# Gathering and transposing the rows of experts 2 to 8: parts of 128 in ten gathers and a block transpose on VectorE, for row gathers and TensorE transposes

## The reference

```python
S = jax.nn.softmax(layernorm(x) @ Wg, axis=-1)          # 1250 x 8
G, I = jax.lax.top_k(St, k)                             # k = 312 nodes for each expert
ex = jnp.take_along_axis(x[:, None], I[..., None], axis=2)       # rows of the normalised x
hmid = gelu(ex @ W1[e] + b1[e])                         # 312 x 512 by 512 x 1024, erf form
out = hmid @ W2[e] + b2[e]                              # 312 x 1024 by 1024 x 512
new_x = zeros.at[I].add(G[..., None] * out);  x = x + new_x
```

## Time and profile before

| | |
|---|---|
| median of 3 runs | 1441.53 us (1441.02 to 1441.79) |
| profiled execution's own time | 1442.35 us |
| its span | 1440.5 us |
| granted TensorE clock, mean over the span | 0.951 of full speed |
| PE busy | 1323.8 us, 92% |
| VectorE busy | 1027.4 us, 71% |
| ScalarE busy | 816.6 us, 57% |
| GpSimd busy | 799.3 us, 55% |
| expert stage | 1116.5 to 1440.5 us |

### The profile page before, as it was taken

One profiled execution on the slowest core, in us unless ns is written; L12 is line 12 of the kernel. 1 busy time (PEld: TensorE's weight loads), 2 busy tenths in 40 slices (PEclk: granted clock), 3 DMA queues, 4 the chain that ended last, 5 costly groups with the idle time before them and its releaser, 6 DMA issues. The chain is left out here.

```text
span 1440.5 us, 26692 instructions
## 1 busy us (share of the span) xinstructions
PE 1323.8 (92%) x7075; PEld 791.9 (55%) x7075; DVE 1027.4 (71%) x2512; ACT 816.6 (57%) x2049; POOL 799.3 (55%) x843
## 2 busy tenths in 40 slices
PE   5786799999999999999999999999962799999997
PEld 1463456656555556555555555555561455555553
DVE  7869589999999899999999999998776311111110
ACT  3769667777777777777777777777550111111111
POOL 5258577777777777777777777777200122222211
PEclk7689899999999999999999999999995799999998
DMA  7315033444443444444443333434452155555421
GB/s 246 162 44 162 20 113 113 123 130 123 126 127 110 129 124 127 127 132 136 123 115 109 110 114 109 115 109 112 65 189 71 58 164 163 163 163 162 145 37 18
DMA packets 65870, 172.45 MB, mean 120 GB/s; under 512 B 14260, under 2 KB 22820, under 8 KB 65191
## 3 DMA queue, kind: packets, MB, share of 16 engines
q0 software_dynamic: 43424, 105.53, 27.9%
q1 hardware_dynamic: 22398, 66.38, 13.4%
HBM read 148.53 MB, written 18.08 MB: 116 GB/s over the span
## 5 line engine op out<-in xcount | busy, mean ns | idle before, releaser
L1130 PE MATMUL PS<-prod,oneh 128*64 128x256 f32 x2052 | 469.6, 382 | 4.0 <-DVE region_s L944 2.0
L564 POOL DMA_INDIRECT recs<-rec_d,inv_i x342 | 323.2, 945 | 113.0 <-issue 81.0
L575 POOL DMA_INDIRECT gath<-table_d,recs x342 | 323.5, 946 | 106.0 <-issue 78.7
L1130 PEld LDWEIGHTS PS<-prod,oneh 128*64 128x64 f32 x2052 | 268.9, 137 | 199.4 <-issue 77.7
L707 ACT ACTIVATE oneh<-oneh,recs 128x64 f32<-128x64 f32 x1026 | 282.2, 338 | 145.7 <-DVE oneh L921 143.8
L1123 PE MATMUL PS<-prod,oneh 128*64 128x256 f32 x1368 | 356.1, 392 | 0.0
L1111 PE MATMUL PS<-wf_sb,h_t 128*128 128x512 f32 x684 | 333.2, 610 | 2.9 <-DVE h_t L907 2.9
L932 DVE TENSOR_TENSOR prod<-PS,gath 128x768 f32<-128x768 f32 x342 | 324.9, 950 | 0.0
L944 DVE TENSOR_TENSOR region_s<-region_s,PS 128x512 f32 x342 | 232.6, 680 | 17.9 <-issue 13.6
L714 ACT COPY PS<-c_rep 128x512 f32<-128x512 f32 x338 | 190.4, 583 | 79.0 <-DVE prod L932 78.6
L930 DVE TENSOR_TENSOR prod<-PS,gath 128x256 f32<-128x256 f32 x342 | 143.9, 421 | 54.6 <-DMA gath<-table_d,recs 38.7
(11 more groups left out here) (264 smaller groups left out, 1503.8 us busy)
## 6 DMA issues: line engine op xcount, KB each, us to landing
region_r<-wu SPq DMA_DIRECT2D x16, 512.0 KB, 4.3
region_r<-wd SPq DMA_DIRECT2D x16, 512.0 KB, 5.6
region_u<-wu SPq DMA_DIRECT2D x16, 512.0 KB, 4.3
region_u<-wd SPq DMA_DIRECT2D x16, 512.0 KB, 5.8
recs<-rec_d,inv_i POOLq DMA_INDIRECT x342, 2.6
gath<-table_d,recs POOLq DMA_INDIRECT x342, 3.3
region_u<-rec_in SPq DMA_DIRECT2D x1, 5168.0 KB, 16.1
rec_d<-region_u SPq DMA_DIRECT2D x1, 5168.0 KB
```

The source lines that it names most:

```text
L564: nc.gpsimd.indirect_dma_start(out=recs[:, q % RING, k, :], out_offset=None, in_=rec_d, in_offset=bass.IndirectOffsetOnAxis(ap=inv_i[:, t: ...
L575: nc.gpsimd.indirect_dma_start(out=gath[:, t % GRING, :], out_offset=None, in_=table_d, in_offset=bass.IndirectOffsetOnAxis(ap=recs[:, q % ...
L1130: return nc.tensor.matmul(to, oneh[:, slot, 1 + i, :], prod[:, slot, P_Q:P_B + i + 1:1 + i, :], start=i == 0, stop=i == 2, skip_group_chec ...
```

## The change

Experts are numbered from 0 in the code. Expert 0 keeps the row gathers and the transposes on PE. For experts 1 to 7:

- Ten gathers replace three. Each fetches 128 pieces of 128 values from `xn_d`, seen as 5000 rows of 128: 32 ranks times four parts, part a of a rank on partition 32a + rank. The index of a partition is 4 x node + part.
- For that, the node index of each rank has to stand on four partitions, 32 ranks to a column. VectorE masks the indices (`idx_b`), PE multiplies them by a constant matrix in two small float32 products with 8 and 2 moving columns (`spread_list`, placed behind row group 0 of the second layer), and VectorE forms `idx_t` (`take_parts`), which GpSimd waits for.
- One VectorE transpose in blocks of 32x32 turns the gathered parts into `ex_t`, straight from SBUF to SBUF, in place of 12 PE transposes and four copies.
- To make the blocks land where the first layer wants them, `xn_d` holds a row's features in another order: value m x 4 + k is feature k x 128 + m. ScalarE writes it so; expert 0's transposes read every fourth column.
- The constant matrix, the masks and the part numbers are made by eleven VectorE instructions at the start of the node stage. `ex_t` has 320 columns a slot, of which 312 are read.

```diff
@@ buffers
+BLOCK = 32
+GROUPS = -(-CAP // BLOCK)
+SLOTS = GROUPS * BLOCK
+        ex_parts = region_x[:, 0:2 * RCH * HID].rearrange("p (a h) -> p a h", a=2)[:, :, 0:GROUPS * FDIM].rearrange(
+            "p a (b h) -> p a b h", b=GROUPS)
+        xn_parts = xn_d.rearrange("n (a h) -> (n a) h", a=PARTS)
+        spread = prod_f[:, 0:2 * P].rearrange("p (n m) -> p n m", n=2)
...
@@ node stage, ScalarE
-                    nc.scalar.activation(xn[:, t, :], x1[:, t, :], ACT.Identity, bias=shift[0:BP, t:t + 1],
+                    nc.scalar.activation(xn[:, t, :].rearrange("p (m k) -> p k m", k=HK),
+                                         x1[:, t, :].rearrange("p (k m) -> p k m", k=HK),
+                                         ACT.Identity, bias=shift[0:BP, t:t + 1],
                                          scale=rstd[0:BP, 2, t:t + 1]).then_inc(n_xn, 1)
@@ node stage, VectorE
+                for part in range(PARTS):
+                    link(nc.vector.memset(part_of[part * BLOCK:(part + 1) * BLOCK, :], float(part)))
+                for n, (at, groups) in enumerate(((0, PARTS), (2 * P - ROW_AT[2], GROUPS - 2 * PARTS))):
+                    rows = ident[:, at:at + groups * BLOCK]
+                    link(nc.vector.tensor_reduce(spread[:, n, 0:BLOCK], rows.rearrange("p (q j) -> p j q", q=groups), AX.X,
+                                                 ALU.add))
+                    link(nc.vector.tensor_copy(spread[:, n, BLOCK:].rearrange("p (a j) -> p a j", j=BLOCK),
+                                               spread[:, n, 0:BLOCK].unsqueeze(1).to_broadcast([P, PARTS - 1, BLOCK])))
+                    link(nc.vector.tensor_reduce(own[:, 2 * PARTS * n:2 * PARTS * n + groups],
+                                                 rows.rearrange("p (q j) -> p q j", q=groups), AX.X, ALU.add))
+                link(nc.vector.tensor_copy(own[:, PARTS:2 * PARTS], own[:, 0:PARTS]))
@@ expert stage, GpSimd (expert 0: gather_rows, the three gathers as before)
+                def gather_parts(e, slot, first=False):
+                    if not first:
+                        pool.wait_ge(f_txe, HK + e - 2)
+                    hold(pool, l_parts, e, pool_passed)
+                    for b in range(GROUPS):
+                        nc.gpsimd.indirect_dma_start(
+                            out=ex_parts[:, slot, b, :], out_offset=None, in_=xn_parts,
+                            in_offset=bass.IndirectOffsetOnAxis(ap=idx_t[:, slot, b:b + 1], axis=0)
+                            ).then_inc(f_parts[slot], 16)
-                gather(0, 0)
-                gather(1, 1)
-                gather(2, 0)
+                gather_rows()
+                gather_parts(1, 1, first=True)
+                gather_parts(2, 0)
                 add_rows(0, 0)
...
@@ expert stage, VectorE, in take_list
+                    nc.vector.scalar_tensor_tensor(out=idx_f[:, :], in0=ex_list[:, slot, :, 0], scalar=float(BLOCKS),
                                                    in1=ex_list[:, slot, :, 1], op0=ALU.mult, op1=ALU.add).then_inc(l_idx, 1)
+                    dve.wait_ge(l_idx, e + 1)
+                    nc.vector.tensor_tensor(idx_b[:, 0:2 * PARTS].rearrange("p (c q) -> p c q", q=PARTS),
+                                            own[:, 0:2 * PARTS].rearrange("p (c q) -> p c q", q=PARTS),
+                                            idx_f[:, 0:2].unsqueeze(2).to_broadcast([P, 2, PARTS]), ALU.mult)
+                    nc.vector.tensor_scalar(idx_b[:, 2 * PARTS:], own[:, 2 * PARTS:], idx_f[:, 2:3], None, ALU.mult
+                                            ).then_inc(l_own, 1)
+                def take_parts(e, slot):
+                    dve.wait_ge(l_spread, e)
+                    nc.vector.scalar_tensor_tensor(out=idx_t[:, slot, :], in0=PS[:, 2, REC:REC + GROUPS],
+                                                   scalar=float(PARTS), in1=part_of[:, :].to_broadcast([P, GROUPS]),
+                                                   op0=ALU.mult, op1=ALU.add).then_inc(l_parts, 1)
+                def parts_transposed(slot, turns):
+                    dve.wait_ge(f_parts[slot], 16 * GROUPS * turns)
+                    nc.vector.transpose(ex_t[:, slot, :, :].rearrange("p k (b j) -> p b k j", b=GROUPS),
+                                        ex_parts[:, slot, :, :].rearrange("p b (i k) -> p b k i", k=HK)).then_inc(f_txe, 1)
...
@@ expert stage, VectorE, loop
                         rank_one_hots(2 * i + slot + 2)
-                        transposed(2 * i + slot + 1, 1 - slot)
+                        parts_transposed(1 - slot, i + 1)
                         take_list(2 * i + slot + 2, slot)
+                        take_parts(2 * i + slot + 2, slot)
                         take_gates(2 * i + slot + 1, 1 - slot)
                         biased(2 * i + slot, slot, i)
@@ expert stage, PE
-                                                   ex_rows[0:n, slot, c, k * P:(k + 1) * P], ident[0:n, 0:n])
+                        last = nc.tensor.transpose(PS[:, 6 + k % 2, at:at + n], ex_rows[0:n, 0, c, k:HID:HK], ident[0:n, 0:n])
+                def spread_list(e):
+                    pe.wait_ge(l_own, e + 1)
+                    for n, (at, end) in enumerate(((0, 2 * PARTS), (2 * PARTS, GROUPS))):
+                        last = nc.tensor.matmul(PS[:, 2, REC + at:REC + end], spread[:, n, :], idx_b[:, at:end],
+                                                start=n == 0, stop=True, skip_group_check=True)
+                    last.then_inc(l_spread, 1)
-                        if ahead is not None and f >= FK - HK:
-                            transpose_rows(e + 1, 1 - slot, ahead, f - (FK - HK))
@@ second layer, behind each row group
                         last.then_inc(f_dn, 1)
+                        if c == 0 and listed:
+                            spread_list(e + 2)
...
                 list_of(1)
+                spread_list(1)
                 for k in range(HK):
-                    transpose_rows(0, 0, 0, k)
+                    transpose_rows(k)
```

More of the change, by code:

```diff
@@ L358, in build @@
         l_gate = sem("l_gate")
+        l_own = sem("l_own")
+        l_spread = sem("l_spread")
+        l_parts = sem("l_parts")
         w_up = [sem("w_up0"), sem("w_up1")]
@@ L362, in build @@
         w_bd = [sem("w_bd0"), sem("w_bd1")]
-        f_rows = [[sem(f"f_rows{h}{c}") for c in range(RCH)] for h in range(2)]
+        f_rows = [sem(f"f_rows{c}") for c in range(RCH)]
+        f_parts = [sem(f"f_parts{h}") for h in range(2)]
         f_tx = sem("f_tx")
@@ L413, in build @@
         idx_add = sb("idx_add", [P, 2, RCH], I32)
+        idx_f = sb("idx_f", [P, RCH])
+        idx_b = sb("idx_b", [P, GROUPS])
+        spread = prod_f[:, 0:2 * P].rearrange("p (n m) -> p n m", n=2)
+        own = sb("own", [P, GROUPS])
+        idx_t = sb("idx_t", [P, 2, GROUPS], I32)
+        part_of = sb("part_of", [P, 1])
         def load_up(sp, e, slot, part):
@@ L1472, in _, with gather_rows @@
                 pool.sem_inc(f_free, 2)
-                def gather(e, slot):
-                    pool.wait_ge(f_tx, 4 * e + 4)
-                    hold(pool, l_idx, e + 1, pool_passed)
+                def gather_rows():
+                    hold(pool, l_idx, 1, pool_passed)
                     for c in range(RCH):
                         nc.gpsimd.indirect_dma_start(
-                            out=ex_rows[0:ROWS[c], slot, c, :], out_offset=None, in_=xn_d,
-                            in_offset=bass.IndirectOffsetOnAxis(ap=idx_e[0:ROWS[c], slot, c:c + 1], axis=0)
-                            ).then_inc(f_rows[slot][c], 16)
+                            out=ex_rows[0:ROWS[c], 0, c, :], out_offset=None, in_=xn_d,
+                            in_offset=bass.IndirectOffsetOnAxis(ap=idx_e[0:ROWS[c], 0, c:c + 1], axis=0)
+                            ).then_inc(f_rows[c], 16)
+                def gather_parts(e, slot, first=False):
[7 more added lines that the diff above has]
+                            ).then_inc(f_parts[slot], 16)
                 def add_rows(e, slot):
@@ L1504, in _ @@
                         e = 2 * i + 2 - slot
-                        gather(e + 2, slot)
+                        gather_parts(e + 2, slot)
                         add_rows(e, slot)
                         settle(e)
-                gather(EXPERTS - 1, 1)
+                gather_parts(EXPERTS - 1, 1)
                 for e in range(EXPERTS - 3, EXPERTS):
@@ L1538, in _ @@
             def _(dve):
-                dve.sem_inc(f_txe, 2)
                 dve.sem_inc(f_bias, 3)
@@ L1604, in _, with transpose_rows @@
                 pe.wait_ge(g_list, 1)
-                pe.sem_inc(f_tx, 8)
                 pe.sem_inc(f_dn, 6)
-                def transpose_rows(e, slot, body, k):
+                def transpose_rows(k):
                     if k == 0:
                         for c in range(RCH):
-                            pe.wait_ge(f_rows[slot][c], 16 * body + 16)
```

(9 more changed lines are left out.)

38 lines of the change are left out of this document (20 added, 18 removed).

## The result

| | before | after |
|---|---|---|
| median | 1441.42 us (1441.02 to 1441.79, 4 runs) | 1427.98 us (1427.17 to 1430.71, 4 runs) |
| profiled execution's own time | 1442.35 us | 1428.51 us |
| its span | 1440.5 us | 1426.7 us |

The ratio is 0.9917, with an interval of 0.9904 to 0.993: faster by 13.4 us. The forecast was 1429.5 (1425.5 to 1435.5).

The account below looks back on a forecast made before the run. The prediction took PE, alone in the chain of waits from 1132.35 to 1430.67, as the bound. -16.0 + 3.9 + 0.1 = -12.0 us against the profiled 1442.35 gave 1430.35, or 1429.5 us as the median; range 1425.5 to 1435.5.

Parts of the forecast that it names:

- Transposes leave PE: First layers of experts 0 to 6 lose four groups of three transposes, 2.26 us a layer: -16.0 us together.
- Spread product: Two small products in PE's queue behind row group 0 of the second layer, 0.65 us, six times: +3.9 us.
- Expert 0: Expert 0's stretch to the next first layer: 2.26 us of transposes go, a 0.65 us spread product comes; forecast -1.6.
- the allowed 1.5 us each way: Expert stage's start: if the clock's rise shifts against the work by 3 us, 1.5 us is won or lost.
- Prologue: Before expert 0: its index signal waits for one more small VectorE instruction, +0.1 us; the rest is hidden.
- Gathers: GpSimd's queue: ten gathers for three, about 1.33 us each, ended by T + 22.0 (T: second layer's start); cost 0.
- VectorE's transpose: Block transpose per expert on VectorE, 1.5 to 1.9 us, within 11.9 us of cover: cost 0.
- Spaced access: 16-byte spacing in ScalarE's writes, VectorE's transpose and expert 0's PE transposes: cost 0; if PE's loads double, +1.9 us (chance 0.10).
- Setup: Eleven VectorE instructions before the node stage, about 2.6 us, nearly covered by 2.46 us of idle: cost 0, bound +0.5.
- The tail stays: The tail behind expert 7 holds no gather and so stays as it was: 0.

Follow-up runs that it names:

- transposes_again: Kernel after with twelve unread transposes of a constant put back on PE in the first layers of experts 0 to 6: 1444.09 us, 1.0025 of before.
- spread_again: Kernel after with each pair of small spreading products done four times over: 1437.28 us, 0.9971 of before.
- before_spaced: Kernel before with rows written in the new order and all eight experts' PE transposes reading every fourth column: 1441.32 us against 1439.87, 1.0006.
- after_third: Kernel after, unedited, measured once more in the third session: 1430.16 us, 0.9926 of before.
- block_x8: Kernel after with VectorE's block transpose of each expert done eight times over: 1448.88 us, 1.0055 of before.

## Why the prediction was right

Its mechanism held: PE bounds the expert stage, transposes leave it, and everything added to the other engines up to the last product is hidden. By its steps:

- **Transposes leave PE, -16.0.** Confirmed: first layers of 17.00 us where there were 19.26, and undone by transposes_again, where they make 16.6. It missed 0.10 us a round: the list product without transposes ahead takes 0.74, not 0.84.
- **Spread product, +3.9.** The term that was mis-sized. I took 0.45 for the stretch and 0.2 for a late product behind it, 0.65. Measured: 0.34, and the two row groups 6.97 each against 13.84 together, 0.10 more; 0.44 in all. A further pair in spread_again costs 0.45, which is what I had from the earlier trace rows. So the row was right for the whole price, and the 0.2 came on top of it without need. With the list's 0.10 this is 0.31 us a round, the 35.62 in place of 35.9, and 1.6 us over experts 1 to 5.
- **Expert 0.** Forecast -1.6 as for the others, measured -1.13. PE started 2.6 us earlier and the clock rose only 0.9 us earlier, so more of the first layer ran at half speed. Over the ten profiles of the three sessions that ran at normal length the rise came 7.3 to 10.6 us after PE's start; the allowed 1.5 us each way was about the right size.
- **Prologue, +0.1.** Measured -0.09 for the whole stretch: the landing and the starts around it moved by more than one small instruction, so this term can't be read.
- **Gathers, 0.** 1.26 us each, as the edge stage's rows said. They ended at T + 20.8 (predicted 22.0). Their landings took 2.6 us at the median and 6.5 at most; the last of the ten, which the transpose waits for, had landed by T + 25.9 (allowed 30.1). The adds land up to 8.4 us behind their issue where I had 6.65 (1.65 and 5.0), so that all have landed by 1219.3 and GpSimd is free for at least 10.6 us (predicted 11.7). The view of the adds' line after says it, against the earlier trace rows:

```profile
DMA to landing us min/median/max: 3.7/7.7/8.4
```

- **VectorE's transpose, 0.** Hidden as predicted, but 2.50 us each, above the 1.5 to 1.9 taken and below the upper bound of 3.8: the rate of columns 12 bytes apart did not hold for 16.
- **Spaced access, 0.** The row of 0.13 us for a load of 12-byte spacing misled (one of its four loads is contiguous besides): at 16 bytes it is 0.20, and ScalarE's ten writes grew from 7.15 to 10.75 us, hidden. The cost on the path is 0.1 us, expert 0's transposes 3.66 to 3.77. The rule weighed against the row (the Trainium skill, SBUF — State Buffer, "Door 1: The DMA port swizzle") wants at least two hits on each 16-byte line. The runs agree with it at 16 bytes on all three engines: 1.51 to 2.50 us, 0.80 to 1.25, 0.14 to 0.20. The same note also gives four float32 elements as how far one can stride for free; that is this spacing, and here it was not free.
- **Setup, 0.** VectorE's eleven instructions in the timeline fill the wait that was there; 2.46 us of idle became 0.52, the second wait is unchanged.

```profile
1036.68 0.17 DVE L1297 COPY own<-own 128x4 f32<-128x4 f32 x1
...
1037.82 0.29 DVE L1268 TENSOR_SCALAR gath<-PS 128x125 f32<-128x125 f32 x1 [0.52 <-ACT soft L1224]
...
1039.67 0.29 DVE L1268 TENSOR_SCALAR gath<-PS 128x125 f32<-128x125 f32 x1 [1.23 <-ACT soft L1224]
```

- **"The tail stays", 0; measured +1.9.** The step that failed. I said that nothing behind expert 7 changes because it holds no gather. Its instructions are the same, but the pause before the last add grew from 0.74 to 1.65 us, and the time from that add's end to the span's end from 6.5 to 7.5. The latter rises with the number of indirect DMAs in the whole program: 6.5 us at 732 (before, before_spaced), 7.3 to 7.5 at 781, 7.8 at 782, 8.1 at 851, most of it GpSimd's closing drain. The drain does not rise in proportion (0.94 us for 49 DMAs more, 0.08 for one, 0.49 for the next 69), and that the number is the cause is not shown.
- **Not in the sum: -2.45 before the expert stage.** The node stage's first VectorE work came 2.2 us earlier, ahead of anything that the change touches. The stage's start lay between 1113.0 and 1117.2 in the kernels with the change, whatever the edit, and the kernel before's 1116.75 lies within, so this is spread of single executions, not a gain. The forecast lay 1.5 us over the median and 0.7 under after_third's, and that it is so close is in part luck; the sum of the parts that belong to the change is -13.27 + 1.92 = -11.4, close to its -12.0, by errors that cancel (spread product and list 1.6 too dear in experts 1 to 5, the tail's 1.9 forgotten, expert 0 0.5 too good).

What stays open: why one session ran 200 us longer and reversed the sign, what makes the pause near the end and the longer drain, and what moves the moment of the clock's rise.

## What to carry to other kernels

When one engine stands alone in the chain of waits, price a removed instruction by the difference of two whole stretches with and without it, and not by its own row: the 0.42 us group was worth 0.59 (2.36 / 4). Ask of every added DMA what it does to the program's end too, not only to its queue. Time such a change in more than one session: it was worth 0.7 to 0.9% in all but one, and cost 1.6% in that one, in which VectorE waited some 10 us in every round.

## What was not expected of the hardware

- Four-byte elements 16 bytes apart against contiguous ones: VectorE's transpose of 128x1280 1.51 to 2.50 us, ScalarE's 125x512 write 0.80 to 1.25 us, PE's load of 128x128 0.14 to 0.20 us.
- The time from the last add to the program's end was 6.5 us with 732 indirect DMAs and 8.1 with 851, GpSimd's closing drain in it 3.98 and 5.49. One add near the end was issued 0.9 to 1.0 us late in every kernel with 781 or 782 of them, the 781st each time.
- Waits of PE like those of 3.9 to 4.6 us in block_x8 cost more than themselves: the clock fell to half, and the row group behind took 9.30 to 9.87 us for 6.97.
- The adds' median landing grew from 5.0 us to 7.7 when they were issued back to back behind ten gathers, instead of one by one behind three.
